# First layer's block scores in four 64 x 64 tiles of TensorE, two blocks a step, under orders laid anew

## The reference, cut to what matters

```python
q, k, v = jnp.split(x @ W_qkv.T + b_qkv, 3, axis=-1)       # q is scaled by HD ** -0.5
qb, kb, vb = (to_blocks(q), to_blocks(k), to_blocks(v))     # b, H=16, t // L = 8 blocks, L = 64, HD = 16
attn = jax.nn.softmax(jnp.einsum('bhnld,bhnmd->bhnlm', qb, kb), axis=-1)
out = jnp.einsum('bhnlm,bhnmd->bhnld', attn, vb)
```

## Time and profile before

| | |
|---|---|
| median of 3 runs | 1941.64 us (1941.33 to 1943.31) |
| span of the profiled execution | 1941.7 us |
| TensorE busy | 1911.9 us, 98% |
| VectorE, ScalarE, GpSimd busy | 1093.9, 919.0, 694.8 us (56%, 47%, 36%) |
| chain that ended last | 96% TensorE |

### The profile page before, as it was taken

One profiled execution on the slowest core, in us unless ns is written; L12 is line 12 of the kernel. 1 busy time (PEld: TensorE's weight loads), 2 busy tenths in 40 slices (PEclk: granted clock), 3 DMA queues, 4 the chain that ended last, 5 costly groups with the idle time before them and its releaser, 6 DMA issues.

```text
span 1941.7 us, 30308 instructions
## 1 busy us (share of the span) xinstructions
PE 1911.9 (98%) x11192; PEld 1317.8 (68%) x11192; DVE 1093.9 (56%) x2904; ACT 919.0 (47%) x1970; POOL 694.8 (36%) x769
## 2 busy tenths in 40 slices
PE   8989999999999999999999999999999999999998
PEld 5835655765575666557656655665786888888887
DVE  5767676558556746656585655577534447223221
ACT  5646666556565555655665566454334321111111
POOL 3302334334332433252343324343443433333332
PEclk9989999999999999999999999999999999999999
DMA  3020001000000100010001000050130223333333
GB/s 129 2 87 15 12 1 39 1 23 12 28 23 1 39 1 23 1 39 15 9 13 28 13 10 15 23 176 2 31 85 4 59 73 98 66 76 79 85 76 70
DMA packets 59696, 76.78 MB, mean 40 GB/s; under 512 B 7120, under 2 KB 52824, under 8 KB 59296
## 3 DMA queue, kind: packets, MB, share of 16 engines
q1 hardware_dynamic: 46448, 57.28, 8.9%
q0 software_dynamic: 12288, 16.79, 5.0%
q10 hardware_dynamic: 816, 0.79, 0.1%
HBM read 53.71 MB, written 21.00 MB: 38 GB/s over the span
## 4 chain that ended last, share of the span: by engine, by line
PE 96%; DVE 2%; ACT 1%; DMA 0%; issue 0%; POOL 0%; SPq 0%; ACTq 0%; DVEq 0%; POOLq 0%
PE bank L765 15%; PE bank L982 12%; PE bank L995 11%; PE bank L832 7%; PE bank L887 4%; PE bank L856 4%; PE bank L868 4%; PE bank L781 3%; PE bank L750 3%; PE bank L591 3%; PE bank L900 3%; PE bank L617 3%; PE bank L841 3%; PE bank L712 2%; PE bank L818 2%; PE bank L692 2%
## 5 line engine op out<-in xcount | busy, mean ns | idle before, releaser
L1232 ACT ACTIVATE h<-bank 128x512 f32<-128x512 f32 x128 | 76.3, 597 | 363.9 <-PE bank L982 352.8
L982 PE MATMUL bank<-xin,ew 128*128 128x256 f32 x1024 | 234.3, 381 | 0.0
L995 PE MATMUL bank<-ew,h 128*128 128x256 f32 x1024 | 226.7, 379 | 0.0
L1776 POOL TENSOR_TENSOR s<-s,ri 128x256 f32<-128x256 f32 (+3 forms) x128 | 160.0, 1268 | 156.5 <-DVE ri L1531 156.5
L995 PEld LDWEIGHTS bank<-ew,h 128*128 128x128 f32 x1024 | 194.2, 190 | 27.7 <-issue 1.5
L982 PEld LDWEIGHTS bank<-xin,ew 128*128 128x128 f32 x1024 | 189.5, 190 | 23.4 <-issue 0.2
L1814 POOL DMA_INDIRECT out<-y,indices x64 | 104.2, 1628 | 265.9 <-DVE y L1668 164.9
L1208 ACT ACTIVATE s<-s,mn 128x128 f32<-128x128 f32 (+3 forms) x256 | 141.0, 552 | 109.0 <-DVE mn L1524 108.9
L1509 DVE SCALAR_TENSOR_TENSOR th<-th,bank 128x384 f32<-128x384 f32 (+1 forms) x192 | 104.3, 594 | 112.0 <-ACT th L1199 110.6
L1668 DVE SCALAR_TENSOR_TENSOR y<-bank,gates,gbe 128x256 f32<-128x256 f32 x64 | 31.0, 484 | 238.5 <-PE bank L995 230.1
L832 PE MATMUL bank<-look,term 128*128 128x384 f32 (+3 forms) x512 | 152.7, 438 | 0.0
(11 more groups left out here) (320 smaller groups left out, 3641.3 us busy)
## 6 DMA issues: line engine op xcount, KB each, us to landing
ew<-L_ffn_w SPq DMA_DIRECT2D x24, 1024.0 KB
x1s<-x_scratch SPq DMA_DIRECT2D x8, 512.0 KB
out<-x1s SPq DMA_DIRECT2D x8, 512.0 KB, 2.9
xn_scratch<-n_xn SPq DMA_DIRECT2D x8, 512.0 KB, 2.9
x<-L_attn_x SPq DMA_DIRECT2D x7, 512.0 KB, 3.8
x_scratch<-x SPq DMA_DIRECT2D x7, 512.0 KB, 3.0
wqkv<-w_qkv SPq DMA_DIRECT2D x1, 3072.0 KB, 10.7
wqkv<-L_wmod SPq DMA_DIRECT2D x2, 1024.0 KB, 8.0
```

Of the source, the lines that this page charges most:

```text
L982: mm = te.matmul(banks[i][:, g * 2 * P:(g + 1) * 2 * P], w1[:, kk, (2 * n + g) * P:(2 * n + g + 1) * P], xin[:, kk, :, :].rearrange("p h s ...
L995: mm = te.matmul(banks[i][:, 0:D], ex.h1[:, g, n * P:(n + 1) * P], w2[:, g, :], start=(g == 0), stop=(g == FC - 1))
L1776: done = g.tensor_tensor(sc, sc, b1.ri[u % 2][:, m, :].unsqueeze(2).to_broadcast([P, 2, w]), ALU.mult)
```

## The change

`sc0` becomes one step for two blocks (8 steps of a batch become 4) and takes two PSUM banks. For each half of the rows (h), for two blocks, two channel halves (c) and two parities of heads, one matmul of a 64 x 64 tile with 128 moving columns: 16 matmuls for two blocks, where 4 of 256 columns stood. Rows choose half of the contraction, the parity chooses 64 output partitions, and each h has its own bank. Keys are stored in two copies instead of four, each with other strips of 32 rows zeroed, by a scale of 0 or 1 per row and a bias multiplied by it: two activations of 128 rows for each `kq`. Exponential and sum run over both blocks at once; GpSimd still multiplies block by block. The zeroing of the key tiles goes; a small constant `row` and a bias `bkr` come. All three order texts are new.

```diff
-            i, nth = at[step, b, n, 0]
-            te.wait_ge(drained[i], nth - 1)
-            for c in range(KC):
-                mm = te.matmul(banks[i][:, c * 256:(c + 1) * 256], f.q[:, c, n, :, :].rearrange("p a l -> p (a l)"),
-                               f.k[:, c, n, :, :].rearrange("p r m -> p (r m)"), start=True, stop=True)
-            mm.then_inc(full[i], 1)
+            for h, rows in enumerate(HALVES):
+                i, nth = at[step, b, n, h]
+                te.wait_ge(drained[i], nth - 1)
+                out = banks[i][:, :].rearrange("p (b r c m) -> p b r c m", b=2, r=2, c=KC)
+                for blk in range(2):
+                    for c in range(KC):
+                        for parity, heads in enumerate(HALVES):
+                            mm = te.matmul(out[heads, blk, :, c, :], f.q[rows, c, 2 * n + blk, parity, :],
+                                           f.k[rows, c, 2 * n + blk, :, :], start=True, stop=True)
+                mm.then_inc(full[i], 1)
...
-            for r in range(NR):
-                rows = slice(32 * r, 32 * r + 32)
-                done = a.activation(f.k[rows, n, :, r, :], banks[i][rows, :].rearrange("p (n m) -> p n m", m=LB),
-                                    ACT.Identity, bias=b0.bk[rows, n:n + 1])
+            for r in range(2):
+                done = a.activation(f.k[:, n, :, r, :], banks[i][:, :].rearrange("p (n m) -> p n m", m=LB),
+                                    ACT.Identity, bias=b0.bkr[:, n, r:r + 1], scale=k.const.row[:, r:r + 1])
...
-            a.activation(f.s[n % 2][:, :, :, :], f.s[n % 2][:, :, :, :], ACT.Exp).then_inc(f.sem["exp0"], 1)
+            for h in range(2):
+                i, nth = at[step, b, n, h]
+                a.wait_ge(drained[i], nth)
+            a.activation(f.s[n % 2][:, :, :, :, :], f.s[n % 2][:, :, :, :, :], ACT.Exp).then_inc(f.sem["exp0"], 1)
...
-    g.memset(k.first[0].v[:, :, :, :], 0.0)
-    g.memset(k.first[0].k[:, :, :, :, :], 0.0).then_inc(s["setup_pool"], 1)
+    g.memset(k.first[0].v[:, :, :, :], 0.0).then_inc(s["setup_pool"], 1)
```

Of the orders, the beginning of `HEAD` (old, then new) and the beginning of `PERIOD`:

```diff
-    0stats:0 0silu:0 1stats:0 0wqkv_load:0 0mod_load:0 0x0:0 0norm:0 1norm:0 0cols:0 0setup:0 1x0:0 0mod_load:1
-    0w0_load:0 0cols:1 0feat:0 0rows:0 1feat:0 0kq:0 1mod_load:0 0kq:1 1mod_load:1 0v:0 0bias0:0 0setup0:0
-    0ga0_load:0 1silu:0 0sc0:0 0sc0:1 0wt0:0 0wt0:1 1kq:0 1ga0_load:0 1kq:1 0tp0:0 0sc0:2 0sc0:3 0wt0:2 0wt0:3
+    0silu:0 0wqkv_load:0 0stats:0 0cols:0 0mod_load:1 0x0:0 0norm:0 1stats:0 1x0:0 1norm:0 0mod_load:0 0cols:1 0bias0:0
+    0feat:0 0setup:0 1feat:0 0rows:0 0kq:0 0kq:1 0v:0 0setup0:0 1silu:0 1mod_load:1 0sc0:0 0w0_load:0 0sc0:1 0ga0_load:0
+    0wt0:0 1kq:0 1kq:1 0v:1 0wt0:1 1sc0:0 0tp0:1 0tp0:0 0sc0:2 1wt0:0 0tp0:2 1v:0 0pv0:0 0wt0:2 0tp0:3 0sc0:3 1cols:0
...
-    proj:0.0 +x0:0 proj:0.2 +stats:0 +norm:0 proj:0.3 +ga0_load:0 proj:0.1 proj:1.4 +feat:0 -attend:10 look:0.0
+    proj:0.1 proj:0.0 +stats:0 proj:0.2 +feat:0 +norm:0 turn_vu:0 proj:0.3 +kq:0 +kq:1 look:0.0 -x1_load:0 -weigh:11
```

More of the change, by code:

```diff
@@ L58 @@
[L58 to L62, removed]
@@ L77 @@
+    0turn:10
 """
 PERIOD = """
-    proj:0.0 +x0:0 proj:0.2 +stats:0 +norm:0 proj:0.3 +ga0_load:0 proj:0.1 proj:1.4 +feat:0 -attend:10 look:0.0
[L83 to L91, removed]
@@ new lines @@
+    look:0.1 term:0 +sc0:0 look:0.2 +sc0:1 -attend:10 +v:0 w:0.0 +v:1 +wt0:0 proj:1.2 +wt0:1 +x0:0 proj:0.4 +tp0:1
+    -turn:11 +tp0:0 +tp0:3 +tp0:2 +pv0:0 w:0.1 -attend:11 +ga0_load:0 +pv0:1 su:0 su:1 sw:0 sw:1 -o_out:3 +sc0:2 sc:0
+    +sc0:3 proj:1.3 -out1:0 +wt0:2 turn_vu:1 -out1:1 +wt0:3 proj:1.1 vc:1 weigh:0 +tp0:5 proj:1.4 +tp0:4 -stats_t:0
+    +tp0:7 vc:3 vc:0 +pv0:2 +tp0:6 proj:1.0 turn:0 su:2 sw:2 look:1.0 +bias0:0 sc:1 look:1.1 sc:2 term:1 weigh:1
+    attend:0 +pv0:3 -norm_t:0 w:1.0 vc:2 +out0:0 -feat_t:0 weigh:2 +out0:1 turn:1 su:3 su:4 +stats:1 sw:3 attend:1 sw:4
@@ new lines @@
+    look:1.2 sc:3 +norm:1 sc:4 turn:2 weigh:3 proj:2.0 -gate:0 +feat:1 weigh:4 proj:2.1 +cn1:0 +twist:0 +gc:0 proj:2.2
+    +cn2:0 attend:2 +gc:1 +cn3:0 w:1.1 +gc:2 look:2.0 -softmax:0 +cn4:0 look:2.1 turn_vu:2 proj:2.3 turn:3 +cn1:1
+    proj:2.4 +cn2:1 su:5 sw:5 w:2.0 +cn3:1 o_out:0 sc:5 term:2 +cn4:1 look:2.2 proj:3.3 proj:3.2 su:6 weigh:5 su:7
+    +cn1:2 w:2.1 attend:3 sw:6 sw:7 +cn2:2 turn:4 turn_vu:3 +cn3:2 attend:4 sc:6 turn:5 weigh:6 proj:3.1 +cn4:2 attend:5
+    o_out:1 proj:3.0 turn:6 su:8 sw:8 look:3.0 sc:7 sc:8 weigh:7 +gate0:0 term:3 look:3.1 w:3.0 weigh:8 attend:6 +fin0:0
@@ L96 @@
+    proj:3.4 turn:7 +stats:2 su:9 sw:9 look:3.2 sc:9 w:3.1 attend:7 -probs:0 weigh:9 turn:8 su:10 sw:10 sc:10 o_out:2
+    +norm:2 weigh:10 attend:8 su:11 turn:9 sw:11 sc:11 attend:9 +feat:2 turn:10
 """
 LAST = """
-    7x0:0 7stats:0 5proj:0.0 5proj:0.1 5proj:0.4 5proj:0.3 7norm:0 7ga0_load:0 5proj:0.2 7feat:0 7bias0:0 5turn_vu:0
-    4attend:10 5term:0 5look:0.0 5look:0.1 5look:0.2 4weigh:11 7kq:0 7kq:1 5proj:1.2 4turn:11 7sc0:0 7wt0:0 7sc0:1
-    7wt0:1 5w:0.0 7v:0 4attend:11 7v:1 5w:0.1 7tp0:0 7sc0:2 7tp0:1 7sc0:3 7wt0:2 5vc:0 7wt0:3 5su:0 5turn_vu:1
@@ L239, in all_steps @@
     return order
-PRODUCTS = {"feat": KC, "kq": 2, "v": 1, "sc0": 1, "tp0": 1, "pv0": 1, "setup0": 1, "out0": 1, "gc": 1, "twist": KC,
+PRODUCTS = {"feat": KC, "kq": 2, "v": 1, "sc0": 2, "tp0": 1, "pv0": 1, "setup0": 1, "out0": 1, "gc": 1, "twist": KC,
             "cn2": 1, "cn3": 1, "cn4": 2, "fin0": NT // 2, "vc": 1, "proj": 1, "look": 2, "term": 2, "su": 2, "sc": 2, "turn": 2, "turn_vu": 1, "w": 1,
```

215 lines of the change are left out of this document (113 added, 102 removed).

## The result

The changed kernel takes 1955.38 us (median of 4 runs, 1954.68 to 1956.73) against 1941.55 us for the kernel before on the same chip: ratio 1.0071, 95% interval 1.0057 to 1.0085. It is slower by 13.8 us; the forecast was 6.3 us slower, with a range of 1930 to 1957. The profiled execution of after has a span of 1953.4 us, 11.7 over that of before.

The account below looks back on a forecast made before the run. TensorE, busy 98% of the span, was taken as the bound. Scores -10.7, shape changes +0.9, front +10.1 and steady part +6.0 gave +6.3 on 1941.7: 1948.0 us, own range 1942 to 1954, with rivals 1930 to 1957.

Parts of the forecast that it names:

- rival 2: Score steps: calls start in program order, 7 calls, 1.61 us a step, 1955 us; chance 0.20 including an 8-call case (1958).
- Scores, -10.7: Score steps: upper rows run two calls' time alone, then four more; 1.40 instead of 1.73 us, 32 times, -10.7 us.
- Rival 1: Score steps: all four tiles run together, 0.86 us a step, 1931 us; chance 0.17.
- Start, +0.8: Front: modulation vector m0cT, needed by TensorE's first matmul, now loads behind larger loads; +0.8 us (0 to 3).
- `setup0`, +7.5: Front: w0_load's 20 DMAs now stand behind rows:0, so TensorE waits for them at setup0; +7.5 us (4.5 to 11.5).
- the slow clock, +2.5: Front: TensorE's clock is low after the gap at setup0; +2.5 us (0 to 4).
- Rival 3: Front: w0_load's weights arrive in time, so wait and slow clock vanish (-10), 1938 us; chance 0.18.
- `cols:1`, +3.7: Front: cols:1 of batch 1 now stands ahead of out0, so the chain of batch 0 starts later; +3.7 us.
- `rows` and `twist`: Front: rows leaves a stretch without idle time, -1.9 us; batch 1's twist fills the wait before feat:2, -2.5 (-5 to 0).
- `feat:0`, 1.0 us for each of five batches: Steady part: feat:0 behind three proj steps waits about 1.0 us for its last tile, batches 3 to 7; +5.0 (0 to 8).
- The coupling chain, 0.2 us a period: Steady part: steps between cn4 and the gelu's end may not cover its 7.4 us; 0.2 each, +1.0 (0 to 6).
- `LAST`, nothing but `feat:0` of batch 7: Last batch: the only wait priced was about 1.0 us at feat:0, within the +5.0 for batches 3 to 7.

Follow-up runs that it names:

- Experiment 1: Changed kernel with w0_load of batch 0 moved back right behind mod_load:0, ahead of rows:0: 1945.64 us, ratio 1.0017.
- experiment 8: Changed kernel with cols:1 of batch 1 moved back between out0 and feat:1 of batch 0: 1963.54 us, ratio 1.0113.
- Experiment 6: Kernel before the change, with the second half of its repeated order (no score step in it) in the new sequence: 1948.80 us, ratio 1.0032.
- experiment 5: Code of the changed kernel under the order lists of the kernel before: 2023.85 us, ratio 1.0416.
- experiments 7: Changed kernel with feat:0 behind four proj steps instead of three, proj:0.4 between turn_vu:0 and kq:0, fin0 behind proj:3.4: 1955.83 us.
- 10: Changed kernel with w0_load early and score halves in turn (1929.69 us), plus the period moves of 7 and proj:1.1 ahead of the transposes: 1930.85 us.
- 11: Kernel of 10 with two front twist steps moved: batch 0's ahead of its cn2:0, batch 1's ahead of fin0:0 of batch 0: 1934.78 us.

## Why the prediction was right, and where it was not

The sign and the wide range (1930 to 1957) were right. The time was 7.4 us too low and outside the forecast's own 1942 to 1954; against the span of the profiled execution, which lies 2.0 under the median of the runs, it was 5.4 too low. The time alone would have suited rival 2 (1955), whose mechanism the traces exclude. And the 5.4 are the sum of larger errors: 3.1 for the scores with the changes of shape, -4.6 for the front, 6.9 for all behind it. That they cancel in part is luck. By its steps:

- **Scores, -10.7.** The mechanism was right (one running and one waiting call per tile; the lower rows' first matmul at 0.50 us where 0.43 plus a late load were given), the size was not: 1.52 us a step, not 1.40, so -6.7. What failed is the end of the step. The last matmul starts 1.32 us in, and with its 0.109 us the halves are through at 1.43; the next step, on the full array, starts 0.09 us after that. I had put the change of shape into a count of changes in the whole list, 447 against 441, and so at nearly nothing per score step, while every one of these steps now ends with one. That is 4.0 us of error, 3.1 with the +0.9 of that count taken off.
- **Rivals 1 and 2.** Both are excluded for the order as written. Rival 1 wanted steps of 0.86 us. Rival 2 wanted 1.61, not far from 1.52, but also lower rows that begin after the upper rows' fourth call has begun; they began at 0.50 us and that call at 0.71. Four tiles do run together once the calls alternate: 1.03 us.
- **Start, +0.8.** Not seen. `m0cT` was late (issued at 2.33 us), and the first matmul began at 10.49 us instead of 9.00, but what released it was the load of the modulation weight, 0.7 us after VectorE had the vector ready (9.79). `kq` of batch 0 began at 25.07 all the same, before the 25.28 of the earlier trace rows.
- **`setup0`, +7.5, and the slow clock, +2.5.** Right in every link: SyncE began the loads at 27.93 (28.8 forecast), TensorE went on at 42.36 (42.8), 8.2 us of gap, 2.5 of clock. Experiment 1 shows it. Rival 3 is out. Over the whole front, though, the slow clock was no longer than before: between 0 and 160 us the granted clock is 0.90 in both kernels.
- **`cols:1`, +3.7.** Wrong in sign. I priced the place it left, and not the one it went to, where it fills a wait of the new kernel (experiment 8). `rows` and `twist`: the wait before `feat:2` did shrink by 2.3 us (-2.5 forecast), but 1.8 us before `fin0` and 0.6 at `cn2` of the second cycle came up ahead of it, which I had not named.
- All of the front together: `proj:0.0` of batch 0 began at 153.47 where it was 146.96, +6.5; forecast were 10.1 less 8 x 0.33 for the scores so far, +7.5. But right behind this mark the kernel before was still at the slow clock: its first eight `proj` matmuls took 153.11 - 146.96 = 6.15 us, and 16 took 6.95 in the changed kernel. That gives 2.7 us back, which the term for `twist` had named ("keeps the clock up") and put too low. So the front cost 3.8 us, 5.5 without the scores' 8 x 0.21, and 10.1 were forecast.
- **`feat:0`, 1.0 us for each of five batches.** The mechanism was right: 0.27 idle and 0.60 by which its matmuls are drawn out, as they wait tile by tile (1.64 us for 1.04). It happened in full for four batches, 4 to 7 (3.5 us, not 5.0), and for batch 3 with 0.3:

```profile
684.70 1.38 DVE L1261 TENSOR_SCALAR n_xn<-x,n_mv,n_rstd 128x256 f32<-128x256 f32 x4 [1.56 <-POOL n_rstd L1714]
685.25 1.64 PE L576 MATMUL bank<-ident,n_xn 128*128 128x128 f32 x8 [0.27 <-DVE n_xn L1261]
```

- **The coupling chain, 0.2 us a period.** This step failed. 0.64 us before `cn3` and `cn2` and 0.54 before `fin0` stand there, 1.2 us a period; in the four periods 4.8 us, where 1.0 was forecast. "Of the other reorderings the trace names none with a price" was the mistake: these waits were covered in the old list, so each chain whose distance in the list shrank had to be measured. Experiment 6 shows that the order alone brings them.
- **`LAST`, nothing but `feat:0` of batch 7.** This failed too: 4.4 us, 5.3 without its four score steps' 0.8. It holds 1.9 at the transposes of the second layer's norm (L915), which wait 1.1 us for the norm and are then drawn out, 1.9 in the `look` steps (from the starts of the trace), 0.9 at `feat:0`; TensorE also waits 1.0 us before L860. No experiment undid any of this, so which move in the list brings it stays open. All behind the front is 11.7 - 3.8 = 7.9 us, 12.9 without its 24 score steps' 0.21 each, and 6.0 were forecast.
- **ScalarE, VectorE, GpSimd at nothing.** True of their load. Their latency was left out: under the old lists the kernel is 82 us slower than the one before (experiment 5), and only the new order hides it.

## What to carry to other kernels

Calls to different tiles of TensorE ran together here only as far as their order let them: the order inside a step was worth 15 us, more than the 6.7 that the tiles gave as first written. The loads that SyncE's queue issued behind a step that waits were late by that whole wait, and TensorE paid twice, in the gap and in the clock behind it. In an order with few waits left, four moves of fill work (experiments 7, 8, 10 and 11) each opened another wait: measure what a step covers in its old place and what it will cover in the new one before pricing the move.

## What the runs showed that was not expected

A third call for a tile holds up the calls for the tiles of the other rows, and the second column of the table shows how sharp that is: the step grows by one call's time, 0.218 us, with each call that is issued too many in a row (1.085, 1.303, 1.521). Two in a row against strict alternation costs 0.05 us. And filling waits of 0.3 to 3.8 us with other work did not pay: the three kernels in which that was tried (experiments 7, 10 and 11) were no faster than their bases.
